# The last experts stage computes each token's two experts, dispatched through DRAM, in place of all eight

## The reference

```python
def _L1_ffn_ref(x, Wg, bg, W1, b1, W2, b2):      # E = 8 experts, K = 2, F = 128, H = 512
    gate_probs = softmax(x @ Wg + bg)
    _, top_idx = top_k(gate_probs, 2)
    selected = gate_probs * one_hot(top_idx, 8).sum(-2)
    selected = selected / (selected.sum(-1) + 1e-08)
    h = gelu(einsum('bsf,efh->bseh', x, W1) + b1)
    expert_out = einsum('bseh,ehf->bsef', h, W2) + b2
    return einsum('bsef,bse->bsf', expert_out, selected)
x = _layernorm(x + _L1_ffn_ref(x, ...))          # the last line of the reference
```

## Time and profile before

| | |
|---|---|
| Median of 3 runs | 3573.7 us (3572.91 to 3577.3) |
| Profiled execution: own time | 3574.55 us |
| Profiled execution: span | 3572.8 us |
| TensorE busy, share of span | 86% |
| VectorE | 69% |
| ScalarE | 51% |
| POOL | 29% |
| Mean granted clock of TensorE | 0.944 |
| Last stage | 2695.1 us to the end |

### The profile page before, as it was taken

The page is one execution under the profiler, slowest core; times in us unless marked ns, Lnnn a source line. Parts: engine busy times, 40 slices in busy tenths (PEclk is TensorE's granted clock), DMA queues, the critical chain, the costliest instruction groups (busy, mean ns, idle before and its releaser), DMA issues. The chain is left out here.

```text
span 3572.8 us, 56056 instructions
## 1 busy us (share of the span) xinstructions
PE 3056.3 (86%) x19198; PEld 2331.4 (65%) x19198; DVE 2468.0 (69%) x6146; ACT 1819.2 (51%) x3099; POOL 1028.1 (29%) x2071
## 2 busy tenths in 40 slices
PE   2456847999999995888867999999996999999998
PEld 1325636777777773666655777777764777777776
DVE  5725756777777772788875666766756777777777
ACT  0002313555555552111113666666654888888887
POOL 3210102444444432222212444444442111111110
PEclk9988977999999996999997999999997999999999
DMA  2052002222222211000002222222201000000000
GB/s 29 26 186 59 23 14 32 41 43 42 35 33 39 42 26 33 13 9 12 6 5 37 38 37 37 37 37 33 32 10 48 7 3 6 6 3 6 6 3 9
DMA packets 116249, 102.16 MB, mean 29 GB/s; under 512 B 32780, under 2 KB 78580, under 8 KB 116156
## 3 DMA queue, kind: packets, MB, share of 16 engines
q1 hardware_dynamic: 114108, 98.87, 14.9%
q10 hardware_dynamic: 2048, 2.10, 0.2%
HBM read 37.85 MB, written 10.65 MB: 14 GB/s over the span
## 5 line engine op out<-in xcount | busy, mean ns | idle before, releaser
L1393 PE MATMUL banks<-Kb,Qb 96*128 96x128 f32 (+3 forms) x2048 | 599.1, 348 | 58.1 <-issue 27.2
L1405 PE MATMUL banks<-Qb,Kb 98*128 98x512 f32 (+3 forms) x2048 | 602.5, 356 | 4.8 <-ACT mla_prob L1296 1.0
L1100 DVE TENSOR_REDUCE mha_nm<-banks 128x1 f32<-128x384 f32 (+3 forms) x704 | 421.5, 639 | 184.0 <-PE banks L1397 170.3
L1296 ACT ACTIVATE mla_prob<-banks 128x512 f32<-128x512 f32 x640 | 376.5, 598 | 311.5 <-PE banks L1405 303.2
L1100 DVE TENSOR_REDUCE mla_nm<-banks 128x1 f32<-128x384 f32 (+3 forms) x704 | 420.0, 638 | 159.7 <-PE banks L1397 146.2
L1296 ACT ACTIVATE mha_prob<-banks 128x512 f32<-128x512 f32 x640 | 375.6, 598 | 270.5 <-PE banks L1405 257.6
L1393 PEld LDWEIGHTS banks<-Kb,Qb 96*128 96x128 f32 x2048 | 364.6, 195 | 215.4 <-issue 159.3
L2045 DVE TENSOR_TENSOR moe_hl<-moe_h,moe_hh 128x512 fp32r<-128x512 f32 x512 | 344.6, 690 | 158.2 <-ACT moe_h L2125 141.5
L2124 ACT ACTIVATE moe_hh<-banks,moe_b 128x512 fp32r<-128x512 f32 x512 | 353.2, 690 | 119.7 <-PE banks L2148 80.9
L1405 PEld LDWEIGHTS banks<-Qb,Kb 98*128 98x128 f32 x2048 | 334.9, 193 | 46.5 <-issue 6.9
L1215 POOL TENSOR_SCALAR_AFFINE_SELECT mla_prob<-mla_prob 128x256 f32<-128x256 f32 (+1 forms) x640 | 237.8, 379 | 405.2 <-PE banks L1393 379.6
(11 more groups left out here) (418 smaller groups left out, 6181.6 us busy)
## 6 DMA issues: line engine op xcount, KB each, us to landing
conv_tz<-conv_kernel SPq DMA_DIRECT2D x16, 1024.0 KB, 6.7
Kb<-mla_kh SPq DMA_DIRECT2D x32, 256.0 KB, 5.0
Qb<-mla_qh SPq DMA_DIRECT2D x128, 64.0 KB
Kb<-mha_kh SPq DMA_DIRECT2D x32, 256.0 KB, 5.6
Qb<-mha_qh SPq DMA_DIRECT2D x128, 64.0 KB
X<-L_attn_idx SPq DMA_DIRECT2D x16, 256.0 KB, 2.8
gate_yt<-conv_out SPq DMA_DIRECT2D x32, 128.0 KB, 2.7
Kb<-mla_kl SPq DMA_DIRECT2D x16, 256.0 KB, 6.7
```

What stands on the lines that cost most here:

```text
L1100: dve.tensor_reduce(nm[:, g % 2, h:h + heads, j], ps[:, bank1(g, k), 0:heads * w].rearrange("p (h k) -> p h k", h=heads), axis=AX.X, op=AL ...
L1296: act.activation(prob[:, g % 2, k, :], ps[:, S2 + k % 2, :], ACT.Exp, scale=HD ** -0.5).then_inc(s2_free, 1)
L1393: one = pe.matmul(ps[:, bank, x * w:(x + 1) * w], Qb[0:MROW, u, g, h + x, j * P:(j + 1) * P], Kb[0:MROW, u, g, 0:w], start=(x == 0), stop= ...
L1405: last = pe.matmul(ps[:, S2 + k % 2, at:at + w], Kb[0:MROW + 2, u, grp, kb * P:(kb + 1) * P], Qb[0:MROW + 2, u, grp, h, kb * P:L], start=T ...
```

## The change

The last stage is rewritten. The sequences form two groups of 8. For each group the router's logits of all its tokens are made first, then VectorE chooses the two best experts in one pass over [128, 32, 8] values (`route`), running counts and a product with a triangular matrix give each chosen (token, expert) pair a slot (`positions`): the pairs of an expert take whole tiles of 512 slots. With 2 x 4096 pairs and 8 experts that is at most 23 tiles a group (`TILES`), 46 in all. POOL scatters each token's row of 128 features to its two slots in a DRAM tensor, with indirect DMAs of 128 rows: 4 blocks x 2 choices a sequence, 64 a group. The expert that owns each tile is a number in SBUF (`own`).

The split weights of the experts are written once to a DRAM tensor `expert_rows` (8224 bytes a partition an expert: high and low halves of both matrices and both biases). The tile loop is straight-line code over 46 tiles. For each SP loads the 512 slots (256 KB), reads the owner into a register and loads that expert's rows (1.05 MB) into one of three buffers. TensorE, ScalarE and VectorE do the same four units as before. The tile's result is evacuated with its bias, transposed back, copied to `yt` and stored to DRAM. After the last tile of a group POOL gathers each token's two result rows (8 indirect DMAs a sequence), and VectorE weighs and adds them to `X`, with layernorm (`combine`, `norm`); group 0's are placed in tiles of group 1, group 1's come after the last tile. The softmax's power on POOL is now an exponential on ScalarE. The slots are filled with zeros beforehand, 1 MB for each sequence from SP in the SwiGLU stage.

```diff
+CLEAR = 4 * L
@@ swiglu_experts_stage, SP
                         load(i * 2 + u, u)
+                        sp.dma_start(slots_d[bass.ds((i * 2 + u) * CLEAR, CLEAR), :].rearrange("(p k) c -> p (k c)", p=P),
+                                     io["c_zero"]).then_inc(cleared, 16)
@@ gelu_experts_stage
+        RING, LAG, BUFS = 4, 3, 3
+        GROUPS = ((0, 8), (8, 8))
+        TILES = [(2 * n * L + E1 * (L - 1)) // L for _, n in GROUPS]
+        TURN = dict(pe=1, act=1, dve=2)
+        EVAC, BACK, KEEP = 3, 0, 1
+        for q, (_, n) in enumerate(GROUPS[:-1]):
+            for j in range(n):
+                COMBINE[FIRST[q + 1] + 4 + j * (TILES[q + 1] - 4) // n] = (q, j)
@@ SP
+                for e in range(E1):
+                    store_rows(e)
+                    if e + 2 < E1:
+                        load_raw(e + 2)
+                def load_tile(g):
+                    q, i = group_of(g)
+                    if g == 0:
+                        sp.wait_ge(cleared, NB * 16)
+                    if i == 0:
+                        sp.wait_ge(own_ready, c.next(own_ready))
+                        sp.wait_ge(scattered[q], GROUPS[q][1] * BLK * 2 * 16)
+                    if g >= BUFS:
+                        sp.wait_ge(w_free, c.next(w_free))
+                    sp.dma_start(xg[:, g % BUFS, :, :],
+                                 slots_d[g * L:(g + 1) * L, :].rearrange("(k p) c -> p k c", p=P)).then_inc(tin[g % BUFS], 16)
+                    e = sp.value_load(own[0:1, g:g + 1], min_val=0, max_val=E1 - 1)
+                    sp.dma_start(f32(wt[:, g % BUFS, :]), wd[e]).then_inc(tin[g % BUFS], 16)
+                for g in range(BUFS):
+                    load_tile(g)
+                for g in range(ALL):
+                    if g + BUFS < ALL:
+                        load_tile(g + BUFS)
+                    store_tile(g)
+                    if g in COMBINE:
+                        store_out(*COMBINE[g])
@@ VectorE
+                def combine(q, j):
+                    n, p = GROUPS[q][0] + j, j % 2
+                    dve.wait_ge(gathered[p], c.next(gathered[p], 2 * BLK * 16))
...
+                def evacuate(g):
+                    dve.wait_ge(o_ready, c.next(o_ready))
+                    link(dve.tensor_scalar(ob[:, :], ps[:, OB + g % 2, :], f32(wt[:, g % BUFS, B2:B2 + 1]), None, ALU.add))
+                    dve.sem_inc(ob_ready, 1)
+                    dve.sem_inc(w_free, 1)
+                for q, (first, n) in enumerate(GROUPS):
+                    for j in range(n):
+                        low_x((TB, BT)[s % 2], s % 2)
+                        s += 1
+                    route(q)
+                    if q == 0:
+                        weights(0)
+                        weights(1)
+                    positions(q)
+                    if q == 0:
+                        for e in range(2, E1):
+                            weights(e)
+                low_x(TB, 0)
+                for g in range(ALL):
+                    for m in range(H1B):
+                        k = (g * H1B + m) % RING
+                        dve.wait_ge(h_ready, c.next(h_ready))
+                        dve.tensor_tensor(hl[:, k, :], h[:, k, :], f32(hh[:, k, :]), ALU.subtract).then_inc(hid_ready, 1)
+                        if m == TURN["dve"] and g + 1 < ALL:
+                            low_x(TB, (g + 1) % 2)
+                        if m == EVAC and g >= 1:
+                            evacuate(g - 1)
+                        if m == KEEP and g >= 2:
+                            keep(g - 2)
+                        if m == 0 and g in COMBINE:
+                            combine(*COMBINE[g])
+                        if m == EVAC and g in COMBINE:
+                            norm(*COMBINE[g])
@@ GpSimd
+                pool.wait_ge(cleared, NB * 16)
+                for q, (first, n) in enumerate(GROUPS):
+                    pool.wait_ge(slot_ready, c.next(slot_ready))
+                    for j in range(n):
+                        for b in range(BLK):
+                            for a in range(2):
+                                t = BLK * j + b
+                                pool.indirect_dma_start(
+                                    slots_d, bass.IndirectOffsetOnAxis(slot[:, q, a, t:t + 1], 0),
+                                    X[:, first + j, b, :], None).then_inc(scattered[q], 16)
+                for q, (first, n) in enumerate(GROUPS):
+                    pool.wait_ge(res_ready, c.next(res_ready))
...
+                                pool.indirect_dma_start(
+                                    gb[:, j % 2, a, b, :], None, res_d[q],
+                                    bass.IndirectOffsetOnAxis(back_slot[:, q, a, t:t + 1], 0)).then_inc(gathered[j % 2], 16)
+                        if j:
+                            root((j - 1) % 2)
@@ TensorE
+                def transpose_tile(g):
+                    pe.wait_ge(tin[g % BUFS], c.next(tin[g % BUFS], 32))
+                    transposes(TB, [xg[:, g % BUFS, b, :] for b in range(BLK)]).then_inc(t_ready, 1)
+                for k in range(ALL * H1B):
+                    g, m = divmod(k, H1B)
...
+                    three(ps[:, FB + k % RING, :], w[:, W1H + m * P:W1H + (m + 1) * P],
+                          w[:, W1L + m * P:W1L + (m + 1) * P], xth[:, g % 2, :], xtl[:, g % 2, :]).then_inc(f_ready, 1)
+                    if k >= LAG:
+                        second_products(k - LAG)
+                    if m == TURN["pe"] and g + 1 < ALL:
+                        transpose_tile(g + 1)
+                    if m == BACK and g >= 2:
+                        back(g - 2)
```

More of the change, by code:

```diff
@@ new lines, in gelu_experts_stage @@
+        trib, oneb = N.sb("trib", [P, P], BF16), N.sb("oneb", [P, P], BF16)
+        lg, pr, ex, eq, sel1, sel2, pos = (N.sb(n, [P, MOST, E1]) for n in ("lg", "pr", "ex", "eq", "sel1", "sel2", "pos"))
+        m1, m2, den = (N.sb(n, [P, MOST]) for n in ("m1", "m2", "den"))
+        took, run = N.sb("took", [P, MOST, E1], BF16), N.sb("run", [P, 2, MOST + 1, E1], BF16)
+        need, ends, base, part = N.sb("need", [P, E1]), N.sb("ends", [P, E1]), N.sb("base", [P, E1]), N.sb("part", [P, E1, E1])
@@ L1888, in gelu_experts_stage @@
[L1888 to L1908, removed]
+        ob, yt = N.sb("ob", [P, L]), N.sb("yt", [P, 2, BLK, C])
@@ L1929, in _ @@
+                for j in range(GROUPS[-1][1]):
+                    store_out(len(GROUPS) - 1, j)
                 sp.wait_ge(stored, NB * 16)
@@ L2064, in _ @@
-                low_x(0)
-                logits()
-                weights(0)
-                for step in range(3):
-                    gate(step)
-                low_rows(0)
-                weights(1)
-                walk(dve, c, tile)
-                add_expert((NB - 1) % 2, E1 - 1)
-                residual(NB - 1)
-                norm(NB - 1)
+                        last = dve.tensor_scalar(X[:, n, b, :], r[:, p, b, :], mv[:, p, b, 0:1],
+                                                 rstd[:, p, b:b + 1], ALU.subtract, ALU.mult)
@@ L2076, in _ @@
+                keep(ALL - 2)
+                evacuate(ALL - 1)
+                keep(ALL - 1)
+                q, n = len(GROUPS) - 1, GROUPS[-1][1]
+                for j in range(n):
+                    combine(q, j)
+                    if j:
+                        norm(q, j - 1)
+                norm(q, n - 1)
             @block.gpsimd
@@ new lines, in _ @@
+                s = 0
+                for q, (first, n) in enumerate(GROUPS):
+                    T = n * BLK
+                    for j in range(n):
+                        high_x((TB, BT)[s % 2], s % 2)
+                        s += 1
+                    act.wait_ge(lg_ready, c.next(lg_ready))
+                    act.activation(pr[:, 0:T, :], pr[:, 0:T, :], ACT.Exp).then_inc(pr_ready, 1)
+                    if q == 0:
+                        for e in range(E1):
+                            weights(e)
@@ L2173, in second_bias @@
[L2173 to L2187 removed]
+                        tok, at = slice(b * P, (b + 1) * P), E1 * (BLK * j + b)
```

513 lines of the change are left out of this document (260 added, 253 removed).

## The result

The changed kernel takes 3707.8 us (median of 4 runs, 3690.1 to 3716.8) against 3573.4 of the kernel before, run beside it on the same chip: ratio 1.037, 95% interval 1.032 to 1.041. It is slower by 134 us. The forecast was 3591, with a range of 3440 to 3720: the time lies inside the range, 117 us above the single number.

A forecast was written before the change was run, and what follows sets the result against it. TensorE alone bounded the last stage. The new stage summed 143 us to tile 0, 9 + 615 in the tile loop, then 18 + 2.7, 83 + 12 and 11: 894 against 877.7, so 3591 us, range 3440 to 3720.

The forecast's parts named there:

- TensorE bounds the stage before; 541 us would go without other limits: Last stage: only TensorE sets its 877.7 us; 46 tiles replace 128 pairs, 82 x 6.6 = 541 us would go.
- Rival A: Tile loop: loads are hidden and TensorE bounds it, period 6.9 us, 3.6 per combine, total 3302 us; chance 0.09.
- The serial loop: one load in flight: Tile loop: each load waits for the previous tile's release; period 6.6 + 7.7 = 14.3 us, 43 loads, 615 us.
- landing: Tile loop: the 1.05 MB expert weights take 5.4 us from issue, 3.5 of it transfer at 300 GB/s.
- chain: Tile loop, load's landing to buffer release: 6.0 us at upper clock, 8.3 at lower, 7.7 taken.
- Owner's number, 0.7 us: Tile loop: SP's read of the expert number, between 0 and 2.3 us, taken as 0.7.
- Indirect DMA 1.3 us: POOL's scatters and gathers: 1.3 us each, between 0.43 and 2.3; 64 take 83 us.
- The rule against the change: POOL's scatters: descriptors cannot be written while VectorE holds the shared port pair, so scatters beside VectorE work cost more than alone.
- rival C: POOL bounds both ends: an indirect DMA costs 2.2 us, 58 us more on scatters and on last gathers, 3707 us; chance 0.23.
- Tile 0 at t = 143: Preparation: scatters land at 136 us from stage start, group 1's routing ends at 133, first load 6.6; tile 0 at 143.
- First three tiles 9 us, then 14.3 each: Tile loop's start: first three loads come at once, 9 us to the first wait, then a 14.3 us period.
- Tail: After the loop: 18 us and last store 2.7, then gathers 83 and roots 12, then 11 to the end at 894.

The follow-up runs named there:

- e10: Changed kernel with a fourth weight and token buffer and POOL waiting for its scatters to land after every sixteen: 3310.7 us, ratio 0.929 to the kernel before.
- e1: Changed kernel with four buffers for weights and tokens instead of three, nothing else: 3409.1 us, ratio 0.955 to the kernel before.
- e4: Changed kernel with 16 extra unused matmuls filling TensorE's pause before the transposes in tiles 3 to 45: 3635.2 us, ratio 1.021 to the kernel before.
- e3: Changed kernel with SP reading the expert number before waiting for the buffer, not between the two loads: 3638.0 us, ratio 1.020 to the kernel before.
- e12: Changed kernel with 48 one-column memsets on idle POOL, moving its later instructions by 48 places: 3613.2 us, ratio 1.014 to the kernel before.
- e2: Changed kernel with group 1's 64 scatters started only after VectorE evacuated tile 7: 3676.5 us, ratio 1.031 to the kernel before.
- e6: Changed kernel with POOL waiting for its eight scatters to land after each sequence, both groups: 3631.2 us, ratio 1.018 to the kernel before.
- e9: Changed kernel with four buffers and POOL waiting for landing after every eight scatters: 3317.4 us, ratio 0.931 to the kernel before.
- e5: Changed kernel with group 1's scatters issued four at a time, released by evacuations of tiles 1 to 16: 3665.4 us, ratio 1.027 to the kernel before.
- e11: Changed kernel with group 1's 64 scatters sent as plain 64 KB transfers to consecutive rows from POOL's queue: 3612.8 us, timed once.
- e8: Changed kernel with 80 extra unused ScalarE copies written out one after the other beside group 0's scatters: 3726.9 us, timed once.
- e7: Changed kernel with 80 extra unused ScalarE copies in a loop beside group 0's scatters: 3770.9 us, timed once.

## Why the prediction came out as it did

- **TensorE bounds the stage before; 541 us would go without other limits.** Right in kind: with loads overlapped (e10) a tile takes 7.4 us (7.9 with the combines), 0.5 above the 6.9 taken for TensorE's work. Rival A's 3302 is the price of the change with hidden loads, and e10 measured 3311. That they lie so close is in part luck: in e10 tile 0 comes 13 us later after the stage's start than forecast, and the stage starts 12.6 us earlier.
- **The serial loop: one load in flight.** Right; e1 shows it by removing it. The period was 14.76 for 14.3. Its terms: issue to transposes 7.3 (forecast 6.6), of which 1.3 from tokens' issue to weights' issue (forecast 1.1) and 6.0 for the landing (forecast 5.5); chain 7.3 (forecast 7.7), means over tiles 5 to 45. e4 confirms that the chain is at the lower level for the most part; the chain at the upper is 5.7, not 6.0.
- **Owner's number, 0.7 us.** Right: 0.72 less between the two issues in e3, 30 us over 41 tiles. The rest of e3's gain is not the read itself: 0.2 us a tile in the chain, with the clock, and the 0.3 of landing left open above.
- **Indirect DMA 1.3 us.** 1.26, on POOL alone and beside VectorE. Group 0's scatters start at t = 54 (50) and take 83 us (83).
- **The rule against the change (the Trainium skill, "SBUF — State Buffer", section "SBUF: two separate sides"), and rival C.** Not borne out here: median and minimum are 962 and 957 ns for scatters that run beside splits and routing, 955 and 943 for gathers. In e12, where the stop does not keep VectorE idle (busy 32.1 of 81 us beside group 0's scatters), they are 958 and 954. No run shows scatters beside a VectorE that is busy throughout. Rival C's time was met by another mechanism.
- **Tile 0 at t = 143: this step failed**, it was 166. Both strands that I gave (scatters, then weights and routing of group 1) were of the right length, and without the stop (e12) tile 0 starts at t = 144.9. The step took each strand to run at its own pace beside the other. I had looked for what the scatters take from each other's queue and from VectorE, and put what they do to all the other engines at nothing.
- **First three tiles 9 us, then 14.3 each: failed at tiles 1 to 4 for the same reason**, 105.9 for 37.6; 42.7 in e12.
- **Tail.** Forecast 18 + 2.7, then 83 + 12, then 11. Measured 20.2 to the first gather (3588.35), 89.3 until the last one ends (3677.7), 10.6 to the end.

That the change is slower does not hang on the stop: e12 is without it and still 45 us slower than the kernel before. That 3708 still lies inside the range, 12 us below its end, is luck: no bound of the range was worked out with a stop in it. With the stop taken out, the same sum is +20 us off in e12's profiled span, 3608.8 for 3589: +2 to tile 0, +5 to tile 4, 41 x 0.76 = +31 in the loop (period 15.06), -7 in the tail, -12 because the stage starts earlier. The loop is slower there than in the changed kernel (14.76); most of that is the landing, 6.4 us for 6.0, and its cause is open.

**What stays open.** Why POOL's code position decides. Shown are: the stop goes with the scatters in time (e2), is absent where the scatters have pauses (e6, e9, e10, group 1's in e5), absent with POOL's program moved by 48 instructions or ended otherwise (e12, e11), and in neither of its stretches in the changed kernel does an instruction block arrive; in e8 an instruction of ScalarE then costs 0.70 us. Every pause is also a wait put into POOL's program, which moves its later instructions, and e12 shows that a move alone can take the stop away. So whether the pauses help as pauses is not shown; no kernel had pauses with the instructions left in their places. That a block fetch of POOL, or of another engine behind POOL's, is blocked by the descriptors of the scatters fits the missing blocks, but not that looped code crawls too and crawls before the block is due (e7); it is only argued. Whether the recording of instructions takes part can't be told either: every time here comes with a recorded span.

## What to carry to other kernels

Count the loads in flight from the release order, not from the number of buffers: with three buffers and a release only two units ahead of the need, a kernel that moves 110 GB/s waits for its loads, and a fourth buffer is worth 290 us. A loop that waits also loses TensorE's clock, and here that was a further 1.6 us in each round of 14.8. Where a chain of waits reads "issue" or "unknown queue" for tens of us, look whether it falls beside a series of indirect DMAs and whether the queues of kind "instruction" carry anything in that stretch. Then try a wait for landing after every sixteen of them, or a shift of POOL's code; here either took the stop away, and why is open.

## What the hardware showed that I had not expected

- Beside 64 indirect DMAs on POOL the other engines can come nearly to a halt for 50 to 75 us, and whether they do depends on 48 instructions in POOL's own program that cost nothing themselves (+134 against +45 us).
- After pauses of 4.3 to 7.1 us TensorE's products started at the lower level in 40 of 41 rounds (0.63 us each in the changed kernel); with 3.8 us of the pause filled by matmuls they started at the upper one (0.40).
- An indirect DMA of 128 rows of 512 bytes costs POOL 1.26 us, a plain one of the same 64 KB 0.54.
